# Reordering the attention stage of a gated cross-attention kernel: turns of two pairs, and six key units ahead of the values

## The reference

```python
q = (layernorm(x) @ Wq), k = (ctx @ Wk), v = (ctx @ Wv)        # [32, 64, 32 heads, 128]
score = einsum('bqhd,bkhd->bhqk', q, k) / sqrt(128) + position_bias
probs = softmax(where(mask, score, -inf)), 0 where masked
ctx2  = einsum('bhqk,bkhd->bqhd', probs, v)
x = x + tanh(g_xattn) * (ctx2 @ Wo)
xf = layernorm(x)
inter = xf @ c1.T @ c2.T                                        # [., 1792], blocks of 32
idx = argmax of each block of 32
h = relu(w1[idx] . xf);  x = x + tanh(g_ffn) * (h @ w2t[idx])
```

## Time and profile before

| | us |
|---|---|
| median of 3 runs | 1881.39 |
| lowest, highest | 1880.97, 1882.59 |
| profiled execution, its own time | 1879.62 |
| its span, first to last instruction | 1877.8 |
| PE (matmul) busy | 1850.2, 99% |
| DVE busy | 1075.3, 57% |
| POOL busy | 966.5, 51% |
| ACT busy | 699.1, 37% |
| mean granted TensorE clock | 0.995 |

### The profile page before, as it was taken

One profiled execution on the slowest core, in us unless ns is written; L12 is line 12 of the kernel. 1 busy time (PEld: TensorE's weight loads), 2 busy tenths in 40 slices (PEclk: granted clock), 3 DMA queues, 4 the chain that ended last, 5 costly groups with the idle time before them and its releaser, 6 DMA issues.

```text
span 1877.8 us, 37912 instructions
## 1 busy us (share of the span) xinstructions
PE 1850.2 (99%) x15304; PEld 1593.4 (85%) x15304; DVE 1075.3 (57%) x1746; ACT 699.1 (37%) x1773; POOL 966.5 (51%) x766
## 2 busy tenths in 40 slices
PE   8999999999999999999999999999999989999999
PEld 7899988899998888888878888888888878888887
DVE  5334466333345455334357666777767787776763
ACT  4223333333233333333345555555555422222221
POOL 5666688866668888778724343343433121111110
PEclk9999999999999999999999999999999989999999
DMA  5455565644455554467658878798786640000000
GB/s 180 167 181 175 187 205 191 211 154 146 152 177 186 191 186 168 163 220 251 221 219 347 323 288 324 279 378 317 313 323 253 238 187 23 23 28 23 29 12 17
DMA packets 129693, 359.51 MB, mean 191 GB/s; under 512 B 12016, under 2 KB 53360, under 8 KB 118512
## 3 DMA queue, kind: packets, MB, share of 16 engines
q1 hardware_dynamic: 129520, 357.09, 53.1%
HBM read 229.11 MB, written 127.93 MB: 190 GB/s over the span
## 4 chain that ended last, share of the span: by engine, by line
PE 75%; DVE 3%; DMA 1%; issue 1%; ACT 1%; SPq 0%; DVEq 0%
PE bank L1439 21%; PE bank L1441 21%; PE bank L1440 21%; PE bank L1506 3%; PE bank L1542 3%; PE bank L1522 2%; PE bank L1663 1%; PE bank L1640 1%; DMA x_tile<-in_x 1%; DVE attn_sum L1248 1%; ACT scores L863 1%; DMA x_tile<-x 0%; DVE attn_sum L1244 0%; PE bank L1619 0%; DVE attn_t_lo L1227 0%
## 5 line engine op out<-in xcount | busy, mean ns | idle before, releaser
L1439 PE MATMUL bank<-tokens_hi,wkq_hi 128*128 128x512 f32 x888 | 346.9, 391 | 4.4 <-DVE tokens_lo L1043 2.8
L725 POOL TENSOR_TENSOR wkq_lo<-raw_wkq,wkq_hi 128x768 fp32r<-128x768 f32 x126 | 284.2, 2276 | 124.6 <-ACT wkq_hi L827 124.4
L1441 PE MATMUL bank<-tokens_hi,wkq_lo 128*128 128x512 f32 x888 | 345.7, 389 | 0.0
L1440 PE MATMUL bank<-tokens_lo,wkq_hi 128*128 128x512 f32 x888 | 345.6, 389 | 0.0
L1439 PE MATMUL bank<-wv_s_hi,tokens_hi 128*128 128x256 f32 x896 | 255.5, 285 | 3.9 <-POOL wv_s_lo L725 3.9
L1441 PE MATMUL bank<-wv_s_hi,tokens_lo 128*128 128x256 f32 x896 | 254.7, 284 | 0.0
L1440 PE MATMUL bank<-wv_s_lo,tokens_hi 128*128 128x256 f32 x896 | 254.7, 284 | 0.0
L1439 PE MATMUL bank<-wo_hi,attn_t_hi 128*128 128x512 f32 x512 | 206.0, 402 | 2.3 <-DVE attn_t_lo L1227 2.3
L1439 PEld LDWEIGHTS bank<-tokens_hi,wkq_hi 128*128 128x128 f32 x888 | 166.7, 188 | 40.0 <-issue 4.2
L1441 PE MATMUL bank<-wo_hi,attn_t_lo 128*128 128x512 f32 x512 | 200.2, 391 | 0.0
L1440 PE MATMUL bank<-wo_lo,attn_t_hi 128*128 128x512 f32 x512 | 199.6, 390 | 0.0
(11 more groups left out here) (146 smaller groups left out, 3714.4 us busy)
## 6 DMA issues: line engine op xcount, KB each, us to landing
k_t<-c SPq DMA_DIRECT2D x128, 256.0 KB, 2.4
v_by_token<-c SPq DMA_DIRECT2D x128, 256.0 KB, 2.3
q_t<-c SPq DMA_DIRECT2D x128, 256.0 KB, 2.3
kt<-k_t SPq DMA_DIRECT2D x16, 2048.0 KB, 9.4
qt<-q_t SPq DMA_DIRECT2D x16, 2048.0 KB, 13.9
v<-v_by_token SPq DMA_DIRECT2D x16, 2048.0 KB, 12.0
raw_wkq<-in_wk SPq DMA_DIRECT2D x32, 512.0 KB, 4.1
raw_wv<-in_wv SPq DMA_DIRECT2D x16, 1024.0 KB, 5.7
```

Of the source, the lines that this page charges most:

```text
L725: pool.tensor_tensor(lo, job_raw(r)[:, a:b, :], hi.bitcast(F32), ALU.subtract)\
L1439: pe.matmul(o, a[0], b[0], start=first_mm, stop=False, skip_group_check=not grouped)
L1440: pe.matmul(o, a[0], b[1], start=False, stop=False, skip_group_check=not grouped)
L1441: return pe.matmul(o, a[1], b[0], start=False, stop=last_mm, skip_group_check=not grouped)
```

## The change

1. `UNITS`: six key units, not four, stand ahead of the values of half 0 (and the tokens of half 1 are prepared two units later).
2. The attention order becomes turns `q` of two duos, a = 2q and b = 2q + 1. On PE a turn is: values of a and b; scores of b + 2 and b + 3; output slot 2a - 2; transposes of a + 2; output slots 2a - 1, 2a, 2a + 1; transposes of b + 2. Duos 0 to 3 and the end have orders of their own. DVE and ACT are reordered to match.
3. The banks of the attended values are now four (two for each parity of the duo), and the transposes of a duo use one of the same banks as the values of that parity. `probs_t` in SBUF has two buffers, not one. A duo's values so wait for the copy of its own transposes and for `clo` of two duos earlier.
4. To make room, the low half of a kept piece is written over its raw piece; the load of the piece after next into that buffer therefore also waits for the store of the kept piece (a new wait on SP).
5. On SP, kt, qt and bias of iteration it + 2 are issued at slots 3, 4, 5 and not at 4, 6, 7; the store of a kept piece stands ahead of the loads of its slot.
6. At the end, the first four selectors of the feed-forward part stand between output slots, and the last six output slots follow each other.

Of the two `probs_t` in the diff, the first is ACT's copy of the transposes, the second is PE's transposes.

```diff
-UNITS = ([("k", 0, u) for u in range(4)] + [("v", 0, u) for u in range(16)] +
-         [("k", 0, u) for u in range(4, 16)] + [("k", 1, u) for u in range(4)] +
+UNITS = ([("k", 0, u) for u in range(6)] + [("v", 0, u) for u in range(16)] +
+         [("k", 0, u) for u in range(6, 16)] + [("k", 1, u) for u in range(4)] +
-SET_FROM = {1: 20, 2: 52, 3: 64}
+SET_FROM = {1: 22, 2: 52, 3: 64}
-SCORE_BANK, PT_BANK, PV_BANK, WO_BANK = (7, 0), (3, 2), (4, 5), (1, 6)
+SCORE_BANK, PV_BANK, WO_BANK = (7, 0), ((3, 5), (4, 2)), (1, 6)
+PT_BANK = (PV_BANK[0][0], PV_BANK[1][0])
...
             def load_piece(n):
                 if n >= 2:
                     sp.wait_ge(*split_done(n - 2))
+                    if PIECES[n - 2][0] == "kept":
+                        sp.wait_ge(kept_out, 32 * (PIECES[n - 2][1] + 1))
...
             def probs_t(d):
-                else:
-                    act.wait_ge(pe_pv, 2 * d)
+                elif d >= 2:
+                    act.wait_ge(pe_pv, 2 * d - 2)
...
             def probs_t(d):
-                else:
-                    pe.wait_ge(act_pt, d - 1)
+                else:
+                    pe.wait_ge(dve_clo, 2 * d - 2)
             def attend(s):
                 elif s % 2 == 0:
-                    pe.wait_ge(dve_clo, s)
+                    pe.wait_ge(dve_clo, s - 2)
...
+            attend_pair(0)
+            project_out(0, heads)
+            probs_t(1)
+            attend_pair(1)
+            scores(3)
+            project_out(1, heads)
+            probs_t(2)
+            project_out(2, heads)
+            probs_t(3)
+            for q in range(1, TURNS - 1):
+                a, b = 2 * q, 2 * q + 1
+                attend_pair(a)
+                attend_pair(b)
+                if q == 1:
+                    scores(4)
+                    scores(5)
+                else:
+                    scores(b + 2)
+                    if b + 3 < DUOS:
+                        scores(b + 3)
+                    project_out(2 * a - 2, heads)
+                if q == 1:
+                    project_out(2 * a - 1, heads)
+                    probs_t(a + 2)
+                else:
+                    probs_t(a + 2)
+                    project_out(2 * a - 1, heads)
+                project_out(2 * a, heads)
+                if q == 1:
+                    scores(6)
+                project_out(2 * a + 1, heads)
+                probs_t(b + 2)
+            attend_pair(DUOS - 2)
+            attend_pair(DUOS - 1)
+            f_transpose_x(0)
+            f_transpose_x(1)
+            project_out(SLOTS - 6, heads)
+            project_out(SLOTS - 5, heads)
+            low_rank(0)
+            project_out(SLOTS - 4, heads)
...
```

More of the change, by code:

```diff
@@ L60 @@
 DUOS = SLOTS // 2
+TURNS = DUOS // 2
 PIECE = 1024
@@ L391, in dest @@
             if kind == "kept":
-                return [t[:, :] for t in kept]
+                return kept[:, :], raw[piece_no[("kept", i)] % 2][:, :].bitcast(F32R)
             if kind == "c1":
@@ L645, in _ @@
                 for n in range(NP):
+                    if PIECES[n][0] == "kept" and PIECES[n][3] + 2 == s:
+                        store_kept(PIECES[n][1])
+                for n in range(NP):
                     lead = {"wo": 4, "kept": 3}.get(PIECES[n][0], 1)
@@ L984, in _ @@
                         hi_piece(n)
-                if d == DUOS + 1:
-                    for k in range(4):
-                        sel(1, k)
+            exps(2)
+            chi(0, 0)
+            chi(0, 1)
+            exps(3)
+            probs_t(1)
+            exps(4)
+            chi(1, 0)
+            chi(1, 1)
+            exps(5)
+            probs_t(2)
+            exps(6)
+            exps(7)
+            split_hi(0)
+            split_hi(1)
+            probs_t(3)
+            for q in range(1, TURNS):
+                a, b = 2 * q, 2 * q + 1
+                more = q + 1 < TURNS
+                if more:
+                    exps(2 * a + 4)
+                chi(a, 0)
+                chi(a, 1)
+                if more:
+                    exps(2 * a + 5)
+                    probs_t(a + 2)
+                else:
+                    fx_hi(0)
+                    fx_hi(1)
+                split_hi(a)
+                if more:
+                    exps(2 * b + 4)
+                chi(b, 0)
+                chi(b, 1)
+                if more:
+                    exps(2 * b + 5)
+                split_hi(b)
+                if more:
+                    probs_t(b + 2)
+            for t in range(2):
+                for k in range(4):
+                    sel(t, k)
             fx_hi(2)
@@ L1370, in _ @@
                         split(n)
-                if d == DUOS - 6:
+            scores(2)
+            clo(0, 0)
+            clo(0, 1)
+            scores(3)
+            probs(2)
+            probs(3)
+            scores(4)
+            scores(5)
+            add_wo(0)
+            probs(4)
+            clo(1, 0)
+            clo(1, 1)
+            probs(5)
+            splits(0)
+            add_wo(1)
+            scores(6)
+            scores(7)
+            add_wo(2)
+            probs(6)
@@ new lines, in _ @@
+            probs(7)
+            splits(1)
+            for q in range(1, TURNS):
+                a, b = 2 * q, 2 * q + 1
+                more = q + 1 < TURNS
+                if more:
+                    scores(2 * a + 4)
+                    scores(2 * a + 5)
+                if q > 1:
+                    add_wo(2 * a - 3)
+                clo(a, 0)
+                if more:
+                    probs(2 * a + 4)
+                clo(a, 1)
+                if more:
+                    probs(2 * a + 5)
+                else:
+                    fx_lo(0)
+                    fx_lo(1)
+                if q > 1:
+                    add_wo(2 * a - 2)
+                splits(a)
+                if more:
+                    scores(2 * b + 4)
+                    scores(2 * b + 5)
+                add_wo(2 * a - 1)
+                if more:
+                    probs(2 * b + 4)
+                clo(b, 0)
+                clo(b, 1)
+                if not more:
+                    low_rank(0)
+                add_wo(2 * a)
+                if more:
+                    probs(2 * b + 5)
+                splits(b)
+                if q == TURNS - 3:
```

190 lines of the change are left out of this document (69 added, 121 removed).

## The result

The changed kernel takes **1895.14 us** (median of 5 runs, 1891.82 to 1897.79) against 1881.39 before: ratio 1.0072, 95% interval 1.0059 to 1.0084. It is slower by 0.7%. The forecast was 1869 with a range of 1863 to 1877.5. The profiled execution took 1893.07 (span 1891.2), 13.45 us more than the one before (1879.62), and 26.05 more than the sum of the prediction.

The account below looks back on a forecast made before the run. PE, busy 99%, was taken to bound the kernel. Terms: -11.6 - 0.9 + 0.8 + 1.0 + 4.7 - 5.5 - 1.1 = -12.6 us, so the profiled 1879.62 becomes 1867.0 and the median 1869; range 1863 to 1877.5.

Parts of the forecast that it names:

- Term 1: Mid-attention on PE: fewer changes of kind cut a two-duo turn from 16.46 to 16.05 us; 29 turns, -11.6 us.
- The mode price alone: PE's turn priced only by tile-shape changes, six before and three now at 0.15 each: 0.46 us less a turn.
- Term 4: First value job: six key units remove most of PE's 6.7 us loss there, 1.2 still lost: -5.5 us.
- Term 3: Duos 0 to 3: 34.0 us from first output slot to values of duo 4, before 29.33: +4.7 us.
- The two low clocks: Head of attention: PE at 1.2 GHz after two idle times, costing 1.6 and 1.5 us.
- Term 2: Attention: DVE and ACT cover the turn; sums waiting for x at the change of halves lose more: +1.0 us.
- Turn 30: End of q = 30: DVE has a split of c2 and a gated sum more before the last probabilities: +0.8 us.
- Term 5: End: selectors no longer wait for ACT, the order is shorter, a wait for a tile goes: -1.1 us.
- The other edits: SP's loads and stores: the new wait for a kept store costs nothing, and loads are the same in number.
- The slower one: Rival: qt, behind a kept piece's load on SP, lands late and stops PE's scores: +22 us, 1891; chance 0.06.
- The wait for ACT's copy in every turn: Rival at the values of b: spare time used up, 0.35 us a turn, 29 turns, +10, 1879; chance 0.11.
- the 0.2 us of cover: Values of b: ACT's copy ends 1.29 us after their transposes begin, PE comes after 1.51: 0.2 us to spare.

Follow-up runs that it names:

- e5: The kernel before with only the six key units ahead of the values, attention as it was: 1876.38 us, ratio 0.9970.
- e9: As e1, but the six waits a turn only from turn 4 on, and more in turns 28 to 30: 1879.74 us, ratio 0.9989.
- e4: The changed kernel with qt issued together with kt at slot 3, PE's instructions the same: 1906.52 us, ratio 1.0139.
- e1: The changed kernel with six more waits a turn on PE, on semaphores long passed, between output matmuls: 1881.67 us, ratio 1.0000.
- e2: As e1, with 127 more such waits in the units of projections: 1917.79 us, ratio 1.0191.
- e3: The changed kernel with only the 127 added waits in the units of projections, turns of 505 instructions: 1909.93 us, ratio 1.0155.
- e12: As e11 without any of the added waits, turns of 505 instructions: 1894.22 us, ratio 1.0065.
- e6: The changed kernel, but from iteration 10 on v loads one part in eight and kt one in four (wrong data there): 1884.64 us, ratio 1.0009.
- e10: As e9, with DVE's last probabilities ahead of the sum in turns 13 to 15 and the split of c last in turn 30: 1876.50 us.
- e11: As e10, with ACT's copy of transposes ahead of its part of c (turn 30) and DVE's probabilities ahead of a sum (turn 16): 1877.01 us.
- e8: As e1, but with the six waits a turn only from turn 7 on: 1884.63 us, ratio 1.0012.
- e7: Control: the kernel before with 127 waits in the units and six more in each two duos: 1881.71 us, ratio 0.9998.

## Why the prediction was wrong

By its steps; in brackets what each contributes to the 26.05 us.

- **Term 1, the turn (+0.5): right.** Forecast 16.05, measured 16.07 to 16.10 in turns 4 to 14. The prices of the changes of kind held. The mode price alone (the Trainium skill, "TensorEngine Tiling (Array Packing)", section Key Properties) would have given 16.00; the rows decided rightly for a little more.
- **Term 4, six key units (+0.6): right.** 4.86 for 5.5, and 1.40 lost around unit 5 where 1.2 was put. e5 has it alone: 1876.4.
- **Term 3, the head (-2.2): the waits right, the clock wrong.** 1.87 and 1.94 before the transposes of duos 3 and 4, for 2.0 and 1.5. The two low clocks that were counted (3.1) didn't come in this run; in others (e9 at 983 us) one did.
- **Term 2, the change of halves (+1.8): undersized.** The tile of x was late by 2.5 and DVE's chain passed it on as 3.04 of PE, with half clock for 3.4 us behind it: turns 15 and 16 lose 4.8, before 2.0. It was inside the bounds named.
- **Turn 30 (+2.6): a wait not seen.** The prediction put 0.8 for more work of DVE there. But the split of c on DVE waits 3.6 us for ACT, and ACT 2.2 for an output slot of PE; DVE's sums behind it hold the last output slot (the 1.9 of L1491).
- **Term 5, the end (+3.7): wrong sign.** From the values of duo 62 to the last instruction it is 2.6 longer; forecast was 1.1 less. The transposes of the first tile wait 3.2 us for DVE, and 3.0 and 1.9 stay ahead of those of h: PE's waits there sum to 8.9, before to 7.1. The clock was at half for 13.7 us around 1521 to 1542, before for 10.2.
- **The step that failed (+19.0).** Terms 1 and 2 price the new turn by the changes of kind and by the cover of DVE and ACT, and all else in the turn is put at nothing ("The other edits" look only at SP's loads). PE has a third supplier, its own code, and no term and no rival had it. 17.5 us were lost so in turns 18 to 29, 1.5 in turns 2 and 3, the low clock behind the waits included. Without these 19.0 the sum would have missed by 7, at 1876, within the range.

**The rivals.** The slower one gave 1891, near what was measured, by a mechanism that e4 rules out: the time was right by accident. The trace alone speaks against it: a wait for qt must stand at the first scores of an iteration, not one matmul into a run. The wait for ACT's copy in every turn didn't come: the 0.2 us of cover held.

**How sure.** That the place in the stream decides is shown by e1, e2, e3 and e12, and that what PE waits for is code, by the packets of q8 that start 2.2 to 3.2 us ahead of each of these ends. That traffic sets most of the length is shown by e6, and e4 agrees. Not shown is when exactly a packet is asked for. Three versions beat both kernels, and can't be told apart: e5, e10 and e11, 0.25 to 0.3% under the kernel before. So the six key units alone give as much as all of the reorder with its repairs. The new turn's 11 us is thus still not brought home: in e11 it is spent in the head, at turn 18 and at the end.

## What to carry to other kernels

A reorder that puts PE's shortest instructions together must be priced for its code too: count the instructions in the densest stretch, and compare the time that 256 of them last with the time that a packet of code takes beside the loads then under way (here 2.1 us against 4.7). An idle time "issue" that ends at the same number modulo 256 of PE's stream is that wait, and waits that cost nothing, put between long matmuls, can move it or hold it still. And when stalls come late in a loop whose turns are all alike, look for what drifts: here 505 instructions against 512.

## What the runs showed of the hardware

- A packet of code is 16384 bytes, was moved in 0.9 to 1.5 us during the attention stage, and PE went on 2.2 to 2.9 us after its start in the waits of turns 18 to 29.
- With the queues at 97%, the packet started 2.3 us after PE had begun the 256 instructions ahead of it, and 0.8 us before that with the queues empty. At other places it started up to 5.8 us after it in e8, and 8.0 in e9 (1248 us).
- A wait on a semaphore that is long reached costs PE nothing between 512-column matmuls (e7: 6 a turn, no turn longer than 16.45 but at the change of halves). In the units, 127 of them made the values begin 0.5 us later (e7).
- After idle times of 2.38 and 2.24 us in turns 19 and 21 PE was granted 1.2 GHz for 3.4 us (1.7 us lost each), not after 2.20 in turn 23.
